# Attention and mixture-of-experts layer on one core: exponentials kept in SBUF, the maximum ahead of the preceding weighted sum, another order of the Q, K, V units, the norm in portions

## The chip, the cores and the metric

The kernel runs on one core of a Trainium2 chip. The metric is the device time of one execution in microseconds. Five engines work side by side, each through its own queue in order: TensorE (PE) multiplies, VectorE (DVE) and ScalarE (ACT) do element-wise work, GpSimd (POOL) does element-wise work in SBUF, and SyncE (SP) issues nearly all transfers. They wait for each other by semaphores. PSUM has eight banks of 128 x 512 words.

## The reference

Input x is (4, 1024, 512): four batches, 1024 tokens, width 512. One layer is computed: attention, norm, routed experts with a shared one, norm.

```
qkv = x @ w_qkv                       # 16 heads of width 128
scores = q @ k.T / sqrt(128)
probs = softmax(scores, axis=-1)
values = einsum('bhqk,bhkd->bhkd', probs, v)   # column sums of probs, times v
x = layernorm(x + values @ w_o)
x = layernorm(x + experts(x) + shared(x))      # 32 experts, 4 per token, capacity
```

Note `bhqk,bhkd->bhkd`: the query index is summed over probs alone. So attention needs for each head only the column sums of the softmax matrix (one number per key), which then multiply V.

## The kernel before, in words

All matrix work is done in three passes of split words: an operand is a rounded high part (HI) and the rest (LO = value - HI), and a product is HI.HI + HI.LO + LO.HI (`PASSES`). So every operand of PE has two makers: ACT rounds the high part, and POOL or DVE subtracts it to give the low part.

The attention goes through 64 heads (M = 64; 16 of each of 4 batches), in pairs of heads (`pair`, with `first_half` and `second_half`; in batch 0 `plain`, twice). A head has T = 8 score tiles of 128 queries x 1024 keys. Per tile t, PE makes the scores in two PSUM banks of four (`p_s`, alternating), `max_tile` on DVE takes the negated row maximum, ACT makes the exponential with its row sum, and `add_tile` on DVE takes the reciprocal and adds the row-weighted exponentials into a 128 x 1024 accumulator. What is left over partitions after eight tiles is folded: ACT copies the upper 64 partitions (`upper_cs`), POOL (DVE in batch 0) adds the lower 64 (`fold_cs`), ACT rounds (`hi_cs`), POOL subtracts (`lo_cs`), and PE sums over partitions and spreads the result with a matrix of ones (`spread`, at tile 3 of the next head). DVE multiplies with V (`times_v`), the pair's values are split, and PE multiplies with w_o (`out_tile`), which DVE adds to y (`add_y`).

In between, PE makes Q, K, V of the next heads. In batch 0 by plain products (`project`). Beside them POOL makes sums of weight blocks of later heads (`load_t` on SP, `sum_t` on POOL, `hi_t_sums` on ACT, `lo_t` on POOL, `store_t` on SP, through one buffer `t_own`), which go to DRAM (`w_jobs`); likewise sums of blocks of x (`load_x`, `sum_x`, `hi_x`, `lo_x`, `store_x_step`). In batches 1 to 3 these serve products with seven in place of eight block products (`unit`: P1 to P7 for Q and K of one head, and seven units for V of two heads, AT_V and AT_VE). A unit is 6 matmuls, accumulated in PSUM banks 4 to 7; between units of one bank ACT evacuates a partial result (`evac_u` to e_1, u_2, e_7 in rows_a; `evac_v`), and DVE or POOL adds the others (`add_block`, `add_v`).

The order of the work is written out by hand: each engine's function lists, for each tile t, what it does at that tile; nothing is planned at run time. Buffers in question:

- In batches 1 to 3 `exp_here` (L1406) writes the exponential back into the PSUM banks of the scores, and the weighted sums (L1902 the first of a head, L1905 the others) read them there. So the scores of tile t wait for the weighted sum of tile t - 2 (`dve_p`). In batch 0 `exp_tile` (L1398) writes to SBUF (`ex`, in rows_a), and the scores wait for the exponential alone (`act_e`).
- Two accumulators alternate there: one in `raws`, and `colsum`.
- The first norm of batch b - 1 (its `read_x`: mean and squares; `scale_x` on POOL; `write_x`: scaling; then `store_y`, `reload_y` on SP) is done in the second pair (k = 1) of batch b.

On DVE a tile is, in `first_half` before: add_tile of tile t - 1, then max_tile of tile t.

```
on_pe.wait_ge(dve_p if banked and not (...) else act_e, n * T + t - 1)   # before a tile's scores
```

## Time and profile before

| | us |
|---|---|
| median of 3 runs | 2806.37 (2805.11 to 2806.81) |
| the profiled execution | 2807.86 |
| its span | 2806.3 |
| PE busy | 2653.3 (95%) |
| DVE busy | 2080.3 (74%) |
| ACT busy | 1565.4 (56%) |
| POOL busy | 1300.6 (46%) |

The span runs from the first to the last instruction of the profiled execution. PE's busy time is modelled and overlapping matmuls count once, so 95% doesn't mean that PE issues at its full rate 95% of the time. Heads can be told apart in the trace by the score matmuls of line 2554: 48 to a head.

### The profile page before, as it was taken

How to read it: one execution, taken by the hardware profiler on the slowest of the kernel's cores; microseconds unless marked ns; L12 is line 12 of the kernel's file. 1: busy time of each engine (PE TensorE's matmuls, PEld its weight loads, DVE VectorE, ACT ScalarE, POOL GpSimd, SP SyncE). 2: the span in 40 equal slices, each digit the busy share in tenths (PEclk: the TensorE clock that was granted, in tenths of full speed). 3: DMA queues.
4: the chain of work that ended last, by engine and by line, in shares of the span. 5: the costliest groups of instructions: out<-in, count | busy, mean ns of one | idle time of the engine just before them, and what ended most of it. 6: DMA issues, size and time to landing. Idle time of an engine off the chain costs nothing.

```text
span 2806.3 us, 40617 instructions
## 1 busy us (share of the span) xinstructions
PE 2653.3 (95%) x12450; PEld 2159.3 (77%) x12450; DVE 2080.3 (74%) x3096; ACT 1565.4 (56%) x2627; POOL 1300.6 (46%) x1042
## 2 busy tenths in 40 slices
PE   9888888999899999999999999899999999999998
PEld 7777777877777777777777777677777788788887
DVE  6877777888788888877888888788888787533346
ACT  5555555656665566576565556756656442244434
POOL 3666666635455454544444444444444220266520
PEclk9999999999999999999999999999999999999999
DMA  5454455544534336445333463533334231288954
GB/s 176 136 171 143 142 169 155 169 170 129 166 112 117 113 103 215 115 120 162 110 103 103 117 205 105 173 98 103 106 101 156 82 128 55 68 253 253 249 162 150
DMA packets 351134, 397.51 MB, mean 142 GB/s; under 512 B 132780, under 2 KB 269996, under 8 KB 350496
## 3 DMA queue, kind: packets, MB, share of 16 engines
q1 hardware_dynamic: 340512, 383.92, 44.2%
q0 software_dynamic: 10496, 12.02, 2.3%
q8 instruction: 66, 1.08, 0.2%
q14 instruction: 60, 0.49, 0.1%
HBM read 299.58 MB, written 106.43 MB: 145 GB/s over the span
## 4 chain that ended last, share of the span: by engine, by line
PE 48%; issue 20%; DVE 19%; ACT 7%; POOL 4%; DMA 1%; ACTq 1%; DVEq 0%; SPq 0%; POOLq 0%
PE banks L2485 11%; PE banks L2554 9%; DVE neg_max L1885 8%; PE banks L2588 6%; PE banks L2394 5%; PE banks L2443 5%; PE banks L2472 4%; PE banks L2456 3%; ACT banks L1406 2%; PE banks L2403 2%; DVE raws L1905 2%; DVE inv L1892 1%; DVE colsum L1905 1%; DVE y_sb L1976 1%; POOL w_all L887 1%
## 5 line engine op out<-in xcount | busy, mean ns | idle before, releaser
L2485 PE MATMUL banks<-xt,w_all 128*128 128x512 f32 x3024 | 764.4, 396 | 77.3 <-ACT rows_a L1319 34.1
L2554 PE MATMUL banks<-qk 128*128 128x512 f32 x3072 | 781.6, 390 | 2.3 <-DVE colsum L1905 1.4
L2485 PEld LDWEIGHTS banks<-xt,w_all 128*128 128x128 f32 x3024 | 563.4, 189 | 234.5 <-ACT rows_c L1347 50.2
L1406 ACT ACTIVATE banks<-banks,neg_max 128x1024 f32<-128x1024 f32 x384 | 417.4, 1087 | 526.7 <-DVE neg_max L1885 523.9
L1885 DVE TENSOR_REDUCE neg_max<-banks 128x1 f32<-128x1024 f32 x512 | 623.5, 1218 | 82.3 <-PE banks L2554 80.4
L2554 PEld LDWEIGHTS banks<-qk 128*128 128x128 f32 x3072 | 574.7, 188 | 128.0 <-DVE colsum L1905 4.3
L2588 PE MATMUL banks<-wo_sb,val 128*128 128x512 f32 x1536 | 380.2, 392 | 8.7 <-DVE y_sb L1976 7.0
L2588 PEld LDWEIGHTS banks<-wo_sb,val 128*128 128x128 f32 x1536 | 289.5, 189 | 73.4 <-DVE y_sb L1976 7.9
L2472 PE MATMUL banks<-xt,w_all 128*128 128x512 f32 x1152 | 287.8, 401 | 6.5 <-DVE xt L2105 6.5
L1892 DVE RECIPROCAL inv<-rowsum 128x1 f32<-128x1 f32 x512 | 82.3, 161 | 278.1 <-ACT banks L1406 274.1
L952 POOL TENSOR_TENSOR qk<-rows_a,qk 128x512 fp32r<-128x512 f32 x144 | 186.5, 1295 | 199.9 <-ACT qk L1331 199.9
L2472 PEld LDWEIGHTS banks<-xt,w_all 128*128 128x128 f32 x1152 | 225.0, 195 | 55.4 <-POOL w_all L887 6.5
L899 POOL TENSOR_TENSOR cs<-folded,cs 64x1024 fp32r<-64x1024 f32 x63 | 150.5, 2389 | 221.1 <-ACT cs L1376 221.1
L1398 ACT ACTIVATE rows_a<-banks,neg_max 128x1024 f32<-128x1024 f32 x128 | 143.1, 1118 | 166.6 <-DVE neg_max L1885 166.1
L1905 DVE SCALAR_TENSOR_TENSOR colsum<-banks,inv,colsum 128x1024 f32<-128x1024 f32 x168 | 215.7, 1284 | 7.2
L1905 DVE SCALAR_TENSOR_TENSOR raws<-banks,inv,raws 128x1024 f32<-128x1024 f32 x168 | 215.7, 1284 | 6.4 <-DVE inv L1892 0.6
L939 POOL TENSOR_TENSOR folded<-folded,colsum 64x1024 f32<-64x1024 f32 x24 | 57.5, 2395 | 314.0 <-ACT folded L1368 314.0
L2394 PE MATMUL banks<-xt 128*128 128x512 f32 x768 | 181.8, 392 | 0.9 <-DVE raws L1848 0.5
L1976 DVE TENSOR_TENSOR y_sb<-y_sb,banks 128x512 f32<-128x512 f32 x256 | 168.2, 679 | 14.5 <-PE banks L2588 12.5
L2394 PEld LDWEIGHTS banks<-xt 128*128 128x128 f32 x768 | 142.5, 188 | 31.0 <-issue 1.7
L1905 DVE SCALAR_TENSOR_TENSOR colsum<-rows_a,inv,colsum 128x1024 f32<-128x1024 f32 x105 | 160.6, 1530 | 4.2
L1078 POOL DMA_INDIRECT acc_rows<-rows_b,who x64 | 93.3, 1458 | 92.0 <-DMA acc_rows<-rows_b,who 42.7
(238 smaller groups left out, 3540.2 us busy)
## 6 DMA issues: line engine op xcount, KB each, us to landing
w_all<-w_jobs SPq DMA_DIRECT2D x144, 512.0 KB, 3.7
w_all<-w_jobs SPq DMA_DIRECT2D x72, 768.0 KB, 4.4
w_jobs<-xt SPq DMA_DIRECT2D x96, 256.0 KB, 3.2
x_jobs<-xt SPq DMA_DIRECT2D x48, 448.0 KB, 5.6
xt<-x_jobs SPq DMA_DIRECT2D x21, 1024.0 KB, 6.7
w_jobs<-w_all SPq DMA_DIRECT2D x72, 256.0 KB, 3.5
...
```

The lines of the kernel that those rows point to most:

```text
L899: pool.tensor_tensor(cs[0:HP], folded[:], rounded(cs[0:HP]), ALU.subtract).then_inc(pool_cs, 1)
L952: pool.tensor_tensor(to[:, LO], f32, rounded(to[:, HI]), ALU.subtract).then_inc(pool_ql, 1)
L1398: act.activation(ex[:, t % 2], p_s[:, t % 2], ACT.Exp, bias=neg_max[:, t % 2], accum_out=rowsum[:, t % 2]).then_inc(act_e, 1)
L1406: act.activation(p_s[:, t % 2], p_s[:, t % 2], ACT.Exp, bias=neg_max[:, t % 2], accum_out=rowsum[:, t % 2]).then_inc(act_e, 1)
L1885: dve.tensor_reduce(neg_max[:, t % 2], p_s[:, t % 2], AX_X, ALU.max, negate=True)\
L1905: dve.scalar_tensor_tensor(out=dst, in0=of[:, t % 2], scalar=inv[:, t % 2], in1=dst, op0=ALU.mult, op1=ALU.add).then_inc(dve_p, 1)
L1976: dve.tensor_tensor(y_sb[:, j], y_sb[:, j], p_o[:, j % 2], ALU.add).then_inc(dve_y, 1)
L2394: ins = pe.matmul(p_f(f % 2, r), s_gu[:, a, k, at], parts[:, PARTS_OF[u], b, k], start=(k == 0 and (a, b) == PASSES[0]), stop=(k == KC - 1 ...
L2472: ins = pe.matmul(p_g[:, g % 2], w_sb[:, a, r, c], xt[:, PLAIN_AT[half][c // 2], b, c % 2], start=(c == 0 and (a, b) == PASSES[0]), stop=( ...
L2485: ins = pe.matmul(psum[:, bank], w_slot[pos % 7][:, a, c], x[:, half, c], start=(opens and c == 0 and (a, half) == PASSES[0]), stop=(c == ...
L2554: ins = pe.matmul(p_s[:, t % 2, keys], qk[:, par, Q, a, at], qk[:, par, K, b, keys], start=((a, b) == PASSES[0]), stop=((a, b) == PASSES[-1]))
L2588: ins = pe.matmul(p_o[:, j % 2], val2[:, r, a, at], wo_sb[:, r, b], start=(r == 0 and (a, b) == PASSES[0]), stop=(r == 1 and (a, b) == PAS ...
```

## The change

Nothing is computed otherwise. These things move:

1. Exponentials of batches 1 to 3 go to SBUF (`ex_late`, all of `raws`), `exp_here` is gone, all heads add into one accumulator `colsum`, and the scores wait for the exponential alone. The head's first weighted sum waits for POOL's fold of the head before.
2. On DVE max_tile of tile t comes ahead of add_tile of tile t - 1.
3. The units of Q and K are made in the order P1, P2, P7, P6, P4, P5, P3 instead of P1, P2, P6, P7, P5, P4, P3, with the evacuations and adds that belong to them; V's blocks are (1, 2, 4) early and (0, 3, 5, 6) in the main part instead of (1, 3, 5) and (0, 2, 4, 6). One of ACT's evacuations of V becomes a copy on DVE (`copy_v`).
4. Batch 0: on POOL `lo_t` of the head before and `lo_cs` come ahead of `sum_t`; on SP `store_w` and `load_w` come ahead of `store_t` and `load_t`; ACT rounds the sums at tiles 5 and 0 of the next head instead of 3 and 6.
5. The norm's reads and writes are spread over more tiles, and x's load in that pair comes after the reads, whose unused output now goes to x's buffer.
6. In the last head `spread` moves from tile 3 to tile 5 and `times_v` from 4 to 6.

The diff, cut to its core:

```diff
-    unused_row = raws[:, 2 * NB:3 * NB]
+    ex_late = raws[:].rearrange("p (a s) -> p a s", a=2)
-    colsums = (raws[:, 0:S], colsum[:])
-    QK_UNITS, V_EARLY, V_MAIN = 7, (1, 3, 5), (0, 2, 4, 6)
+    QK_UNITS, V_EARLY, V_MAIN = 7, (1, 2, 4), (0, 3, 5, 6)
-    P1, P2, P6, P7, P5, P4, P3 = range(7)
+    P1, P2, P7, P6, P4, P5, P3 = range(7)
...
         def plain(i, s):                                   # SP
             n = 2 * i + s
+            store_w(n + 1)
+            if n + 2 < H:
+                load_w(n + 2, n + 2)
             if 2 <= n - 1 <= H - 3:
                 store_t(n - 1, 1)
             if 2 <= n <= H - 3:
                 load_t(n, 0)
-            store_w(n + 1)
-            if n + 2 < H:
-                load_w(n + 2, n + 2)
...
         def second_half(b, k):                             # SP
-            if x_too:
+            if x_too and not k1:
                 load_x(b, k + 1, T * b + k + 1)
...
             if k1:
+                on_sp.wait_ge(act_q, 4 * TT * b)
+                load_x(b, k + 1, T * b + k + 1)
                 reload_y(b, 0)
...
         def plain(i, s):                                   # POOL
-            if sums:
-                sum_t(n, 0)
+            if late_sums:
+                lo_t(n - 1, 1)
             if not (is_first(i) and s == 0):
                 lo_cs(n - 1)
             if sums:
-                lo_t(n, 0)
+                sum_t(n, 0)
             if not end:
                 lo_w(n + 2, Q)
+            if x_step:
+                sum_x(0, i + s)
             if s == 0 and not is_first(i):
                 lo_wo(n - 1, 1)
             if sums:
-                sum_t(n, 1)
+                lo_t(n, 0)
             if not end:
                 lo_w(n + 2, K)
-            if x_step:
-                sum_x(0, i + s)
             if sums:
-                lo_t(n, 1)
+                sum_t(n, 1)
...
         def plain(i, s):                                   # ACT
-                if t in (3, 6) and sums:
-                    hi_t_sums(n, t // 6)
+                if t == 0 and (not isinstance(i, int) or 2 <= n - 1 <= H - 3):
+                    hi_t_sums(n - 1, 1)
+                if t == 5 and sums:
+                    hi_t_sums(n, 0)
...
         def first_half(b, k, i):                           # ACT
                 if t == 1:
                     evac_u(i, P1, m, 0)
+                    if k1:
+                        read_x(c, [0, 1])
...
                 if t == 4:
                     hi_val(n - 2, 0, i)
+                    if k1:
+                        read_x(c, [3])
+                        read_x(c + 1, [0])
                 if t == 5:
+                    evac_v(i, 3)
                     hi_block(i, 0, m, 1, 1)
-                    evac_v(i, 3)
...
-                exp_here(n, t)
-                if k1 and t < TT:
-                    read_x(c, [t])
+                exp_tile(n, t, ex_late)
...
         def second_half(b, k, i):                          # ACT
                 if t == 0:
-                    upper_cs(n - 1, colsums[0])
+                    upper_cs(n - 1)
+                    if k1:
+                        read_x(c + 1, [2])
+                        write_x(c, [0, 1])
                 if t == 1:
+                    evac_u(i, AT_S1 + P1, m, 0)
                     if not (b == 0):
-                        evac_v(i, 6)
-                    evac_u(i, AT_S1 + P1, m, 0)
+                        evac_v(i, 5)
+                    if k1:
+                        read_x(c + 1, [3])
+                        write_x(c, [2, 3])
...
-                if k1 and t == 1:
-                    write_x(c)
-                if k1 and t == 5:
-                    write_x(c + 1)
...
         def add_tile(n, t, of, by_pool=True):              # DVE
             if t == 0:
+                if by_pool:
+                    on_dve.wait_ge(pool_f, n - (H - 2))
+                else:
+                    on_dve.wait_ge(dve_cs, n)
+                dve.tensor_scalar(colsum[:], of[:, 0], inv[:, 0], None, ALU.mult).then_inc(dve_p, 1)
...
+        def copy_v(i):
+            on_dve.wait_ge(pe_u, units(i, AT_V + 2))
+            on_dve.wait_ge(dve_v, 2 * (2 * i))
+            dve.tensor_copy(v_sb[:, 1, NB:S], psum[:, 7]).then_inc(dve_ve, 1)
...
         def first_half(b, i):                              # DVE
-                if t == 0:
-                    add_tile(b, n - 1, T - 1, colsums[1], p_s)
-                else:
-                    add_tile(b, n, t - 1, colsums[0], p_s)
                 if t == 2:
                     add_block(i, 0, m, 0)
+                if t == 5:
+                    add_block(i, 0, m, 2)
+                if t == 7:
+                    copy_v(i)
                 max_tile(n, t)
...
                 if t == 6:
                     lo_block(m, 1)
+                if t > 0:
+                    add_tile(n, t - 1, ex_late)
...
         def second_half(b, i):                             # DVE
                 if t == 3:
-                    add_block(i, AT_S1, m, 1)
+                    add_block(i, AT_S1, m, 2)
...
                 max_tile(n, t)
                 if t == 1:
                     add_block(i, AT_S1, m, 0)
+                if t == 2:
+                    add_block(i, AT_S1, m, 1)
                 if t == 4:
                     lo_block(m, 0)
+                if t > 0:
+                    add_tile(n, t - 1, ex_late)
...
             elif j == P5:                                  # PE, qk_unit
-                on_pe.wait_ge(act_qe, 3 * q + 2)
+                on_pe.wait_ge(act_qe, 3 * q + 3)
             else:
-                on_pe.wait_ge(dve_qc, 3 * q + 2)
+                on_pe.wait_ge(dve_qc, 3 * q + 3)
...
         def v_unit(b, i, k):                               # PE
+            elif k < 3:
+                on_pe.wait_ge(act_ve, evacs(i, 3 + k))
             else:
-                on_pe.wait_ge(act_ve, evacs(i, 3 + k))
+                on_pe.wait_ge(dve_ve, i - (PB - 1))
...
         def scores(n, par, t, banked):                     # PE
-            on_pe.wait_ge(dve_p if banked and not (isinstance(n, int) and n == M - 1 and t >= 2) else act_e, n * T + t - 1)
+            on_pe.wait_ge(act_e, n * T + t - 1)
...
         def first_half(b, i):                              # PE
-                for j in {0: (P1,), 1: (P2,), 2: (P6, P7), 3: (P5,), 4: (P4,), 5: (P3,)}.get(t, ()):
+                if t == 5:
+                    v_unit(b, i, 1)
+                for j in {0: (P1,), 1: (P2,), 2: (P7, P6), 3: (P4,), 4: (P5,), 5: (P3,)}.get(t, ()):
                     qk_unit(b, i, 0, j)
-                if t >= 4:
+                if t in (4, 6, 7):
                     v_unit(b, i, t - 4)
```

## Rows read from the trace of the kernel before

**Rows 1.** The page, section 1: busy us, share of the span, instructions.
```profile
PE 2653.3 (95%) x12450; PEld 2159.3 (77%) x12450; DVE 2080.3 (74%) x3096; ACT 1565.4 (56%) x2627; POOL 1300.6 (46%) x1042
```

**Rows 2.** The chain of waits in time order, from 1250 us: start, us, what.
```profile
1260.99 1.37 PE banks L2554 x6
```

**Rows 3.** Windows at heads: length, busy PE, PEld, DVE, ACT, POOL, PEclk, DMA, GB/s.
```profile
80.00:122.50 42.50, 35.17 (x147) 28.37 (x147) 35.51 (x39) 25.08 (x39) 29.43 (x19) 0.92 0.51 149
200.20:233.30 33.10, 33.10 (x148) 27.41 (x147) 27.87 (x37) 20.53 (x31) 22.26 (x18) 1.00 0.46 140
233.30:277.80 44.50, 36.56 (x148) 29.30 (x147) 33.59 (x38) 22.35 (x34) 27.23 (x18) 0.88 0.56 164
464.60:507.80 43.20, 35.25 (x147) 28.44 (x146) 32.08 (x38) 22.28 (x34) 27.24 (x18) 0.92 0.57 169
606.00:639.00 33.00, 27.88 (x118) 21.43 (x118) 25.74 (x33) 21.34 (x34) 20.66 (x15) 1.00 0.32 96
1011.00:1076.80 65.80, 63.40 (x276) 50.98 (x275) 53.29 (x69) 39.52 (x64) 32.16 (x22) 1.00 0.39 110
1207.80:1243.40 35.60, 32.70 (x142) 26.08 (x142) 28.72 (x37) 29.67 (x58) 19.22 (x16) 1.00 0.40 108
1243.40:1284.20 40.80, 34.47 (x136) 27.25 (x135) 26.36 (x33) 26.66 (x47) 18.72 (x37) 0.92 0.56 188
```

**Rows 4.** PE's waits over the whole span: us in total, times, longest.
```profile
PE banks L2564 <- POOL cs L899: 40.8, 6, 7.6
PE banks L2485 <- ACT rows_a L1319: 34.1, 29, 1.8
PE banks L2485 <- ACT rows_c L1347: 30.3, 40, 3.9
```

**Rows 5.** Timeline of batch 0's even head from 233.3 us: start, us, engine, line.
```profile
242.51 1.05 ACT L1376 CAST cs<-folded 64x1024 fp32r<-64x1024 f32 x1 [1.14 <-DVE folded L1920]
...
248.14 0.72 POOL L906 TENSOR_TENSOR rows_c<-rows_c 128x256 f32<-128x256 f32 x1 [6.81 <-DMA rows_c<-in_w_qkv]
...
253.83 1.22 PE L2564 MATMUL banks<-cs,ones 128*128 128x512 f32 x2 [6.81 <-POOL cs L899]
...
254.85 3.62 PE L2472 MATMUL banks<-xt,w_all 128*128 128x512 f32 x8
```

**Rows 6.** Timeline of a second half with the norm.
```profile
737.50 2.92 ACT L1175 ACTIVATE y_sb<-y_sb,n_shift,n_scale 128x512 f32<-128x512 f32 x4
...
740.94 1.01 PE L2485 MATMUL banks<-xt,w_all 128*128 128x512 f32 x2 [3.31 <-ACT rows_c L1347]
```

**Rows 7.** Timeline of an ordinary first half, its last unit and its releaser.
```profile
976.06 0.58 ACT L1347 COPY v_sb<-banks 128x512 f32<-128x512 f32 x1
...
976.69 1.66 PE L2485 MATMUL banks<-xt,w_all 128*128 128x512 f32 x6 [0.39 <-ACT v_sb L1347]
```

**Rows 8.** Groups by line: busy us, mean ns of one, idle before.
```profile
L1905 DVE SCALAR_TENSOR_TENSOR colsum<-banks,inv,colsum 128x1024 f32<-128x1024 f32 x168 | 215.7, 1284 | 7.2
...
L1905 DVE SCALAR_TENSOR_TENSOR colsum<-rows_a,inv,colsum 128x1024 f32<-128x1024 f32 x105 | 160.6, 1530 | 4.2
...
L899 POOL TENSOR_TENSOR cs<-folded,cs 64x1024 fp32r<-64x1024 f32 x63 | 150.5, 2389 | 221.1 <-ACT cs L1376 221.1
```

**Rows 9.** DVE's instructions on rows_a: ns least/median/most, first and last start.
```profile
L1905 DVE SCALAR_TENSOR_TENSOR colsum<-rows_a,inv,colsum x105: 1283/1354/2926, 36.7 to 2214.9; 128x1024 f32<-128x1024 f32 x105
...
L1902 DVE TENSOR_SCALAR colsum<-rows_a,inv x15: 753/753/1600, 32.6 to 2189.0; 128x1024 f32<-128x1024 f32 x15
```

**Rows 10.** Timeline of DVE and POOL around one long weighted sum.
```profile
255.52 2.38 POOL L918 TENSOR_TENSOR xt<-rows_c,xt 128x1024 fp32r<-128x1024 f32 x1 [1.97 <-ACT xt L1294]
...
256.06 2.93 DVE L1905 SCALAR_TENSOR_TENSOR colsum<-rows_a,inv,colsum 128x1024 f32<-128x1024 f32 x1
```

**Rows 11.** Timeline of a tile where DVE waits for the scores.
```profile
245.50 1.52 PE L2554 MATMUL banks<-qk 128*128 128x512 f32 x6
...
247.06 1.23 DVE L1885 TENSOR_REDUCE neg_max<-banks 128x1 f32<-128x1024 f32 x1 [0.68 <-PE banks L2554]
248.20 0.68 DVE L1912 SCALAR_TENSOR_TENSOR qk<-banks,qk 128x512 fp32r<-128x512 f32 x1
```

224 lines of the change are left out of this document (108 added, 116 removed).

## The prediction

> **What bounds the kernel now.** I read the page first: TensorE (PE) is busy 95% of the span [rows 1], so the time can fall only by what PE waits, or by removing matmuls, and this change removes none. Busy time overstates PE, because matmuls overlap, so I priced one matmul from the chain of waits in order of time: six of them pass in 1.37 us [rows 2], 0.2265 us each by the length of undisturbed heads. With that price I cut the attention into heads at the first score matmul and laid windows over them [rows 3] (their matmul counts hold one or two of the neighbours at each edge; I use the program's counts). The reader is to see three kinds of excess there.
> - Batch 0, odd head: 146 matmuls cost 33.1 us and the window is 33.1 us long: no excess. The even head after it has as many and takes 44.5 us. The heads that begin at 80.0, 155.6, 233.3, 310.9, 387.4 and 464.6 us (heads 2 to 12, even) take 262.3 us together (six rows of that view, the first and the last of them shown), against 6 x 33.1 = 198.5: 63.8 us lost.
> - Batches 1 to 3, an ordinary pair of heads: 274 matmuls cost 62.1 us, the window is 65.8: 3.7 us lost, in nearly each of 24 pairs.
> - The pair in which the first norm of the preceding batch is done: 35.6 + 40.8 = 76.4 us, 10.6 more than an ordinary pair, three times (31.8 us). At the first head after batch 0, 116 matmuls cost 26.3 and take 33.0.
>
> From about 2213 us on (experts and last norm) the change touches nothing that PE waits for; I leave that part as it is.
>
> **Part A: order of POOL and SP in batch 0.** In the even heads PE's largest wait of the kernel stands: the spreading matmuls (L2564) wait for POOL's cs, 40.8 us in 6 waits [rows 4]. The stretch shows why [rows 5]: POOL idles 6.81 us until the weight blocks (rows_c) land, since the four subtractions of sum_t stand ahead of lo_cs in its queue; they were loaded late, because SP's load waits for lo_t of the head before, which stood last but one in POOL's queue. PE then idles 6.81 us, and the eight matmuls behind it take 3.62 us, 0.43 each, twice the usual time: the window's granted clock falls to 0.88, so part of them ran at 1.2 GHz, after PE had stood idle. Of such an 11 us, 7 are the wait, 2.8 the slow matmuls, and 1.4 a wait for DVE's y_sb later in the head, which is DVE's backlog from the stall.
> The change puts lo_t of the head before and lo_cs ahead of sum_t. What lo_cs waits for is then ACT's high half of cs, at 9.2 us of the head (242.51 in rows 5), and POOL's work before it: lo_wo until about 7.7, lo_t 2.4 us to 10.1, lo_cs 2.4 us [rows 8] to 12.5. PE wants it after three tiles of 18 matmuls and a score, 66 - 6 = 60 matmuls or 13.6 us. Cover: 1.1 us; it is gone if lo_t comes later. lo_t waits for ACT's rounding, moved to tile 0, that for the second sum_t, that for the load which SP issues only after lo_t of the first block. I step through it: first lo_t ends near 26 us, loads issued to 28, landed near 30.4 (about 4.3 us after the first issue), sum_t 3.2 us and its queue to 34, which is 1 us into the next head, ACT idle then until its exponential at 2.8. So it fits, with little to spare. SP's stores and weight loads, now ahead of the store and load of blocks, take some 5 us of issue at the head's start, when the block store cannot go anyway. POOL is busy 22.3 and 27.2 of 33 and 44 us in such heads [rows 3], 75% when the pair shrinks. I take 0.6 us of new wait per head: 63.8 - 3.8 = **-60 us** (bounds: -64 with none, -35 if half of each wait comes back).
>
> **Part B: norm in portions.** In the pair with the norm ACT is busy 29.7 + 26.7 = 56.4 us against 39.5 [rows 3], so 16.9 us for 16 reading and 8 writing instructions. It isn't the sum that hurts (ACT has 9 us left) but the lumps: four writes in a row, 2.92 us, ahead of one evacuation, after which PE had idled 3.31 us [rows 6]; the granted clock is 0.92 in that head [rows 3]. The change writes two at a time and spreads the reads. The rests that I find, by laying the new order out tile by tile: two reads at tile 4 of the first half put the evacuation that V's second unit needs some 2 us late; two writes and a read at tiles 0 and 1 of the second half cost another 2 to 3; about 1 later. That is 5.5 of 10.6, and no wait long enough to bring the slow matmuls: 3 x 5.1 = **-15 us** (bounds -26 and 0). The load of x now waits for the reads (its buffer takes their unused output); SP holds back only itself, and the transfer has three tiles until hi_x, moved to tile 7.
>
> **Part C: exponentials in SBUF, maximum first, units in another order.** Today's 3.7 us per pair are four waits of PE's unit matmuls for ACT's evacuations (rows_a and rows_c in rows 4), the last of the first half in rows 7. ACT is not full; it holds an exponential ahead of each evacuation, the exponential waits for the maximum, and the maximum stands behind reciprocal and weighted sum of the tile before, which wait for *its* exponential. Max first takes 1.4 us (0.2 + 1.2 of spacing) out of that loop, and two evacuations move ahead in ACT's order. All four waits (0.5 to 1.5 us) go. What is late next? I lay out the new order with: maximum starts 1.56 us after the scores' first matmul (245.50 to 247.06), holds DVE 1.14 (to 248.20) [rows 11]; reciprocal plus sum 1.4; a 512-wide add or copy 0.6 to the next, 0.68 to its end [rows 11].
> - *V's fourth unit* in the first half now waits for copy_v, which DVE does after max 6, lo_block and sum 5: 1.56 + 1.14 + 0.6 + 1.4 + 0.68 + 0.1 = 5.5 us after scores 6 begin. PE is there after scores 6, V's third unit, scores 7: 18 matmuls, 4.1 us. It waits 1.4, and 0.1 to restart. Today's wait at this place is 0.39 [rows 7].
> - *P3 in the second half* waits for the add of P5, now behind max 2, the add of P4 and sum 1: 5.8 us after scores 2 begin, where PE comes at 5.4: 0.4 + 0.1.
> - *DVE's price.* A sum costs 1284 ns from PSUM; from SBUF a head's first one costs 753 [rows 9], but the others take 1530 on average [rows 8], between 1283 and 2926 [rows 9]. The long ones overlap POOL: the one of 2.93 us starts at 256.06 while POOL works until 257.90, and ends 1.09 us after that [rows 10]. So each sum begun under a POOL instruction waits for its end. I take +0.25 us (1530 - 1284) for 14 sums of a pair, -1.06 for the two first ones, +0.68 for copy_v: 53.3 + 3.1 = 56.4 us of DVE in a pair of 65: DVE does not bound. ACT has 26 us a pair free [rows 3] and gives up one copy: nothing there.
> - *Where such a wait meets PE.* lo_cs (2.4 us) runs in the second half about when sum 1 is due; up to 1.2 us on the P3 wait, I take 0.6. In the first half POOL's 1.3 us pieces touch sum 5: 0.2, and P6 behind P1's evacuation 0.2.
> - *Added wait.* One colsum for all heads: the first sum of a head waits for POOL's fold, and max, adds and all of DVE behind it. Last sum, ACT's copy 1.05, fold 2.4: 3.6 us; DVE has max 0, adds and max 1 between, over 3.6 us in both halves. Nothing, or 0.5 if POOL is held.
>
> Sum per pair: 1.5 + 0.5 + 0.6 + 0.2 + 0.2 = 3.0 after, 3.7 to 3.8 before: -0.8, times 24 = **-19 us**. Bounds: all four waits go and nothing comes, -3.3 x 24 = -79; every sum waits like the longest of 2926, the fourth rival's +13 each. I stand nearer the small gain since both new waits follow from the order of DVE alone.
>
> The Trainium skill, page "SBUF — State Buffer", section "Who interferes with whom", has a rule that speaks against this part: a DVE instruction with two SBUF inputs contends with a GpSimd instruction that reads SBUF, with one PSUM operand it doesn't, and the first to start holds the port to its end. The trace agrees on both sides (1284 on average from PSUM, up to 2926 from SBUF). By the row's mean the pair loses 3.5 us of DVE slack, by the rule's worst case that of the fourth rival.
>
> **Part D: edges.** In the first head after batch 0 the scores no longer wait for the weighted sums: of its 6.7 us I take 2.5 back; the last head's spread moves where it waits for nobody: 0.5. **-3 us** (0 to -6).
>
> Sum: -60 - 15 - 19 - 3 = -97. The profiled execution took 2807.86 us (span 2806.3 and 1.56 around it), so 2710.9; the median is 1.5 less: **2709 us**.
>
> **Rivals.**
> 1. *PE's floor in the pairs.* The new waits are hidden after all and pairs take 62.5: 2806.4 - 60 - 15 - 79 - 3 = 2649. For it: max first removes the longest loop. Against: the two sums above. Chance 0.22.
> 2. *The pairs give nothing or lose.* Contention moves the waits for copy_v and P3 over 2 us, where today the slow matmuls appear (3.31 us of idling in rows 6); pairs take 65.8 to 67.8: 2728 to 2776, say 2745. Chance 0.22.
> 3. *Batch 0 keeps half its stall*, as lo_t comes late behind the chain of load, sum and rounding, with 1.1 us of cover: 35 instead of 60, 2734. Chance 0.08.
> 4. *DVE becomes the bound by POOL's port, slower than before.* Place: the 16 sums of a pair. Each waits 1.64 us more (2926 - 1284) at worst, 26 us a pair; 53.3 - 0.4 + 26 = 79 us, +13 x 24 = +317: 3045. It decides from a pair of 69.1 on, where 3.3 x 24 eats A, B and D; that is 16 us of waiting in a pair, 1 us per sum, four times the measured mean; POOL is busier in batch 0, where that mean is from, than in the later pairs (32.2 of 65.8). Chance 0.05.
> 5. *The change doesn't do what it says*: ACT's order holds the exponentials back, and A is hidden by another wait: within 0.2%. Chance 0.02.
>
> The forecast has the remaining 0.41. The range goes from rival 1 to the middle of rival 2: 2645 to 2765; the forecast's own is 2690 to 2725. A difference under 0.2% (5.6 us) can't be told from none here; faster by more: 0.41 + 0.22 + 0.22 + 0.08 = 0.93; same 0.02; slower 0.05.
>
> **What would show it.** A: waits of L2564 for POOL gone from PE's list, even heads at 33 to 34 us, clock 1.00. B: second half of the norm pairs under 38 us. C: PE's units waiting for DVE's v_sb copy about 1.4 us once a pair, and for rows_a's add in the second half; sums from SBUF near 1.5 us mean; exponentials right after maxima; a pair near 65. I am wrong if a pair takes 62.5 (new waits hidden) or over 67 (port), or if even heads of batch 0 stay over 36.

## The result, and the profile after

| | before | after |
|---|---|---|
| median, us | 2805.82 (4 runs) | 2781.43 (4 runs, 2772.5 to 2785.49) |
| the profiled execution | 2807.86 | 2785.49 |
| after / before | | 0.9909 [0.9882, 0.9935] |

The change makes the kernel 24 us faster, a quarter of the 97 us forecast; 2709 was forecast and 2781 lies above the range. The page's section 1 of after, against [rows 1]: DVE gained 80 us of work and POOL 107. PE waits less in sum, but in the profiled executions it has 94 us at half clock (1.2 GHz) against 70 before. After's four runs, 2785.49, 2784.64, 2772.5 and 2778.22 us, were granted 0.984, 0.984, 0.989 and 0.988 of the full clock over their spans; 0.005 of the span is 14 us, so by this estimate most of their scatter of 13 us is the clock, and the profiled run is the slowest of the four.

```profile
PE 2655.4 (95%) x12450; PEld 2179.1 (78%) x12450; DVE 2160.8 (78%) x3120; ACT 1556.8 (56%) x2603; POOL 1407.8 (51%) x1042
```

PE's waits of after over the whole span (us in total, times, longest), against [rows 4]: L2578 is the spreading matmul, L2602 `out_tile`, L2497 a unit, L2568 the scores.

```profile
PE banks L2497 <- DVE v_sb L2017: 49.6, 24, 2.9
PE banks L2578 <- POOL cs L904: 12.8, 5, 2.7
PE banks L2497 <- DVE rows_a L1940: 12.5, 24, 1.2
PE banks L2568 <- POOL qk L957: 11.4, 3, 4.0
PE banks L2602 <- POOL wo_sb L898: 7.6, 4, 3.0
```

The two old waits for ACT's evacuations (34.1 and 30.3 us) are gone, as forecast, the third (11.2 us, for v_sb) as well. The one for POOL's cs has shrunk from 40.8 to 12.8 us and is not gone, and four others have come. Windows of after at heads (columns as in [rows 3]): an odd and two even heads of batch 0, the first head after it, an ordinary pair, the two halves of a norm pair.

```profile
116.70:149.80 33.10, 33.10 (x148) 27.41 (x147) 28.80 (x37) 20.44 (x31) 24.32 (x19) 1.00 0.58 177
149.80:191.70 41.90, 36.45 (x147) 29.33 (x146) 34.12 (x38) 22.21 (x34) 30.98 (x19) 0.92 0.53 157
443.00:485.30 42.30, 36.69 (x148) 29.48 (x147) 34.40 (x39) 22.20 (x34) 31.00 (x19) 0.92 0.51 154
586.70:619.40 32.70, 28.41 (x117) 22.46 (x116) 30.50 (x36) 22.06 (x35) 24.48 (x16) 0.96 0.42 125
988.20:1053.50 65.30, 62.70 (x275) 51.28 (x274) 55.33 (x71) 39.12 (x63) 35.74 (x22) 1.00 0.38 110
1186.50:1225.00 38.50, 32.58 (x142) 25.96 (x140) 32.59 (x41) 29.77 (x58) 22.03 (x25) 0.99 0.40 120
1225.00:1259.10 34.10, 33.46 (x134) 27.14 (x135) 24.84 (x30) 26.25 (x45) 22.51 (x28) 0.91 0.61 201
```

Cutting both traces at the first score matmul of each head puts the 22.8 us by which the spans differ where they belong:

| | before | after | difference | forecast |
|---|---|---|---|---|
| even heads 2 to 12 | 262.3 | 238.9 | -23.4 | -60 |
| rest of batch 0 | 318.6 | 322.0 | +3.4 | 0 |
| three norm pairs | 228.3 | 218.1 | -10.2 | -17 |
| 19 other pairs | 1248.0 | 1255.0 | +7.0 | -15 |
| first pair after batch 0 | 65.7 | 64.1 | -1.6 | -3 |
| start, last heads, the rest | | | +2.0 | -1 |

### The profile page after: what moved, and what is told of

It reads as the page before. It is cut to its first block, busy times and chain, and to the rows that moved or that the text cites. A ratio compares the mean times of both kernels' runs of the same rounds, so it can differ in the third digit from the quotient of the medians.

```text
span 2783.5 us, 40658 instructions
## 1 busy us (share of the span) xinstructions
PE 2655.4 (95%) x12450; PEld 2179.1 (78%) x12450; DVE 2160.8 (78%) x3120; ACT 1556.8 (56%) x2603; POOL 1407.8 (51%) x1042
## 3 DMA queue, kind: packets, MB, share of 16 engines
q8 instruction: 66, 1.08, 0.2%
## 4 chain that ended last, share of the span: by engine, by line
PE 66%; issue 5%; DVE 3%; POOL 1%; ACT 1%; DVEq 0%; ACTq 0%; POOLq 0%
PE banks L2497 21%; PE banks L2568 15%; PE banks L2602 9%; PE banks L2406 6%; PE banks L2455 5%; PE banks L2468 3%; PE banks L2415 3%; PE banks L2330 1%; PE banks L2578 1%; PE banks L2442 1%; DVE rows_a L1940 1%; DVE qk L1949 1%; DVE v_sb L2017 1%; PE banks L2354 0%; DVE colsum L1910 0%
## 5 line engine op out<-in xcount | busy, mean ns | idle before, releaser
L2497 PE MATMUL banks<-xt,w_all 128*128 128x512 f32 x3024 | 760.8, 395 | 66.5 <-DVE v_sb L2017 49.6
L2568 PE MATMUL banks<-qk 128*128 128x512 f32 x3072 | 792.3, 394 | 11.7 <-POOL qk L957 11.4
L2497 PEld LDWEIGHTS banks<-xt,w_all 128*128 128x128 f32 x3024 | 570.6, 190 | 207.0 <-DVE v_sb L2017 59.8
L1407 ACT ACTIVATE raws<-banks,neg_max 128x1024 f32<-128x1024 f32 x392 | 438.5, 1119 | 508.2 <-DVE neg_max L1893 504.9
L2568 PEld LDWEIGHTS banks<-qk 128*128 128x128 f32 x3072 | 584.3, 190 | 136.8 <-POOL qk L957 12.7
L1910 DVE SCALAR_TENSOR_TENSOR colsum<-raws,inv,colsum 128x1024 f32<-128x1024 f32 x343 | 525.3, 1531 | 13.5
L2602 PE MATMUL banks<-wo_sb,val 128*128 128x512 f32 x1536 | 381.0, 392 | 13.9 <-POOL wo_sb L898 7.6
L2602 PEld LDWEIGHTS banks<-wo_sb,val 128*128 128x128 f32 x1536 | 289.4, 189 | 79.1 <-issue 10.7
L944 POOL TENSOR_TENSOR folded<-folded,colsum 64x1024 f32<-64x1024 f32 x49 | 117.3, 2394 | 376.7 <-ACT folded L1378 376.7
L957 POOL TENSOR_TENSOR qk<-rows_a,qk 128x512 fp32r<-128x512 f32 x144 | 204.6, 1428 | 133.1 <-ACT qk L1341 133.1
L1407 ACT ACTIVATE rows_a<-banks,neg_max 128x1024 f32<-128x1024 f32 x120 | 134.1, 1117 | 131.0 <-DVE neg_max L1893 130.1
L1910 DVE SCALAR_TENSOR_TENSOR colsum<-rows_a,inv,colsum 128x1024 f32<-128x1024 f32 x105 | 174.6, 1663 | 4.2
L948 POOL TENSOR_TENSOR val<-rows_b,val 128x1024 fp32r<-128x1024 f32 x48 | 140.7, 2932 | 22.7 <-ACT val L1399 22.7
L1378 ACT COPY folded<-colsum 64x1024 f32<-64x1024 f32 x63 | 66.1, 1049 | 122.3 <-DVE colsum L1910 121.9
## 6 DMA issues: line engine op xcount, KB each, us to landing
xt<-x_jobs SPq DMA_DIRECT2D x21, 1024.0 KB, 10.8
```

The costliest lines, as they stand in the source:

```text
L948: pool.tensor_tensor(val2[:, r, LO], val[:, r], rounded(val2[:, r, HI]), ALU.subtract)\
L957: pool.tensor_tensor(to[:, LO], f32, rounded(to[:, HI]), ALU.subtract).then_inc(pool_ql, 1)
L1407: act.activation(to[:, t % 2], p_s[:, t % 2], ACT.Exp, bias=neg_max[:, t % 2], accum_out=rowsum[:, t % 2]).then_inc(act_e, 1)
L1910: dve.scalar_tensor_tensor(out=colsum[:], in0=of[:, t % 2], scalar=inv[:, t % 2], in1=colsum[:], op0=ALU.mult, op1=ALU.add).then_inc(dve_p, 1)
L2497: ins = pe.matmul(psum[:, bank], w_slot[pos % 7][:, a, c], x[:, half, c], start=(opens and c == 0 and (a, half) == PASSES[0]), stop=(c == ...
L2568: ins = pe.matmul(p_s[:, t % 2, keys], qk[:, par, Q, a, at], qk[:, par, K, b, keys], start=((a, b) == PASSES[0]), stop=((a, b) == PASSES[-1]))
```

## Experiments

All are edits of the kernel after, except `e7_max_first_psum`, an edit of the kernel before. Times are medians, ratios to the kernel before with their interval; "heads" and "pairs" are cut as above.

### 1. The copy of V earlier: `e1_copy_early`

DVE's copy moves from behind the sum of tile 5 to ahead of it.

```diff
@@ DVE, first half
-                if t == 7:
-                    copy_v(i)
                 max_tile(n, t)
...
                 if t == 6:
                     lo_block(m, 1)
+                    copy_v(i)
                 if t > 0:
                     add_tile(n, t - 1, ex_late)
```

> The changed kernel with copy_v done at tile 6, behind lo_block and ahead of the weighted sum of tile 5, instead of at tile 7 behind that sum. Theory (PE waits once a pair for DVE's order max 6, lo_block, sum 5, copy_v): the wait of the unit matmuls for v_sb, 2.1 to 2.3 us once a pair, goes, first halves fall from 34.1 us to about 32, a pair from 65.3 to 63.1; 24 pairs give 50 to 60 us, about 2725. Rival (DVE is the bound through the sums from SBUF, and the wait only moves): the pair stays over 64.5 and the gain is under 20 us, 2762 or more.

Measured: 2753.3 us, 0.9815 [0.9798, 0.9831], 28 us under after. PE's waits:

```profile
PE banks L2567 <- POOL qk L957: 20.7, 6, 5.1
PE banks L2496 <- ACT rows_a L1329: 18.7, 18, 1.1
PE banks L2496 <- DVE rows_a L1940: 14.3, 24, 1.2
```

The wait of 49.6 us is gone and the first halves fall from 34.15 to 31.8 us. But the second halves rise from 31.15 to 32.6: the next unit's evacuation by ACT, which the longer first half had covered, is now late 18 times. So the wait is real, but of the 2.35 us that the first half gains the second gives 1.45 back: a typical pair takes 64.4 us, between the 63.1 expected and the rival's 64.5, and the 28 us lie between the two as well. The pairs that took 66.9 us in after gain most: of the six ordinary ones five now take 64.3 or 64.4. In the norm pairs hardly anything is gained: there the wait for POOL's qk grows from 3.7 to 5.1 us.

### 2. Batch 0's order undone: `e2_batch0_back`

SP, POOL and ACT in batch 0 as in the kernel before, the rest as after.

```diff
@@ POOL, plain
-            if late_sums:
-                lo_t(n - 1, 1)
+            if sums:
+                sum_t(n, 0)
             if not (is_first(i) and s == 0):
                 lo_cs(n - 1)
...
@@ SP, plain
-            store_w(n + 1)
-            if n + 2 < H:
-                load_w(n + 2, n + 2)
             ...                      # store_t, load_t
+            store_w(n + 1)
+            if n + 2 < H:
+                load_w(n + 2, n + 2)
```

> The changed kernel with the order of batch 0 (SP, POOL, ACT) as before. Theory (batch 0 brings 20 us of the whole gain): even heads 2 to 12 take 262 us again instead of 239, the first sixteen heads 581 instead of 561, the whole about 2801. Rival (the order of batch 0 is worth the 60 us that I forecast and something else of the change takes 40 away in batch 0): over 2820.

Measured: 2799.7 us, 0.9978 [0.9968, 0.9988]. The even heads take 262.3 us again and POOL's cs is waited for 40.4 us in 6 waits. Part A is worth 18 us by the medians and 19 by the sixteen heads of batch 0, not 60; the rest of the change is worth the remaining 6.

### 3. The norm in lumps: `e3_norm_back`

```diff
@@ ACT, first half
+                if k1 and t < TT:
+                    read_x(c, [t])
+                if k1 and t in (5, 6):
+                    read_x(c + 1, [t - 5])
@@ ACT, second half
+                if k1 and t < 2:
+                    read_x(c + 1, [2 + t])
+                if k1 and t == 1:
+                    write_x(c)
+                if k1 and t == 5:
+                    write_x(c + 1)
-                ...                  # the same calls one or two at a time
```

> The changed kernel with ACT's reading and writing of the norm at the places of before (one read behind the exponential of each tile, four writes in a row at tiles 1 and 5 of the second half). Theory (portions bring 3.4 us a norm pair): the three norm pairs take about 228 us instead of 218, the whole about 2791. Rival (with maxima ahead ACT has room for the lumps): the three pairs within 3 us of 218, no difference that can be measured.

Measured: 2790.1 us, 0.9949. The three norm pairs take 233.8 us against 218.1: the portions are worth 15.7 us in the new order, where about 10 were expected (8.7 by the medians; batch 0 of this run took 5 us less than after's, with the same code). All of it lies in the second halves, 39.5 us against 34.2; the first ones take 38.4 either way.

### 4. Sum ahead of the maximum, in SBUF and in PSUM: `e4_sum_first`, `e7_max_first_psum`

The first undoes the order of DVE's two instructions in after; the second makes the order of after in the kernel before, whose exponentials are in PSUM. With the two kernels they fill a table of two by two. Within a row only that order differs. The rows differ in more than the place of the exponentials: in after the units come in another order, V's copy is DVE's and there is one accumulator.

```diff
@@ e4_sum_first, both halves
+                if t > 0:
+                    add_tile(n, t - 1, ex_late)
                 max_tile(...)
-                if t > 0:
-                    add_tile(n, t - 1, ex_late)
@@ e7_max_first_psum, both halves
-                    add_tile(b, n, t - 1, colsums[0], p_s)
                 max_tile(...)
+                if t > 0:
+                    add_tile(b, n, t - 1, colsums[0], p_s)
```

> The changed kernel with the weighted sum of tile t - 1 ahead of the maximum of tile t again in batches 1 to 3; exponentials stay in SBUF, the scores wait for the exponential alone, copy_v stands ahead of sum 6 at tile 7, so no longer behind sum 5 and max 7 but behind max 6 and lo_block. Theory (max first shortens the loop that ACT's evacuations hang on, 1.4 us): the waits of unit matmuls for ACT come back, 3 to 4 us a pair, the wait for copy_v goes (-2.3), pairs at 65 to 67, the whole 2775 to 2820. Rival (the loop never mattered, only the order of units and evacuations did): pairs at 63, about 2725.

> The kernel before with one thing of the change: in batches 1 to 3 the maximum of tile t ahead of the weighted sum of tile t - 1, exponentials still in PSUM. Theory (the two parts need each other: with exponentials in PSUM the scores of tile t + 1 wait for the sum of t - 1, now behind max t, 1.56 + 1.14 + 1.4 us after scores t begin, 4.1 and more where an add stands between): pairs at 68 to 76 us instead of 65.8, the whole 2860 to 3050. Rival (max first helps by itself, as ACT's evacuations come earlier): pairs under 65.

Measured: 2871.7 us, 1.0241 [1.0224, 1.0259], and 3044.3 us, 1.0845. An ordinary pair, us:

| | sum first | maximum first |
|---|---|---|
| exponentials in PSUM | 65.8 (before) | 76.6 |
| exponentials in SBUF | 69.9 | 65.3 (after) |

The first was expected at 2775 to 2820 us, with the copy's wait gone, and missed: that wait stayed. The second came in the range expected, its pair just above it. So the maximum first costs 10.8 us a pair in PSUM and gains 4.6 in SBUF. The 4.1 us by which the sum first in SBUF is over the kernel before are not the price of SBUF alone: 2.1 us of each pair are the wait for the copy, which the kernel before leaves to ACT. PE's waits with the sum first in SBUF, then with the maximum first in PSUM:

```profile
PE banks L2497 <- ACT rows_a L1329: 46.6, 32, 2.3
PE banks L2497 <- DVE v_sb L2017: 44.7, 23, 2.1
PE banks L2497 <- ACT rows_a L1357: 13.4, 23, 2.0
```

```profile
PE banks L2554 <- DVE raws L1905: 139.3, 111, 2.1
PE banks L2554 <- DVE colsum L1905: 68.4, 72, 1.4
```

In PSUM the scores of tile t need the bank that the sum of tile t - 2 reads, and with the maximum ahead that sum is late at half of the tiles (201 waits in 384 tiles). In SBUF that tie is gone; but with the sum first a sum that is longer than in PSUM (1475 ns on average) stands ahead of the maximum, the exponential behind it, and ACT's evacuation behind that, and the waits for ACT are back.

### 5. Which queue holds batch 0: `a1_wo_after_cs`, `a2_sp_back`, `a3_wo_before_sum`, `a4_wo_all`

```diff
@@ a1_wo_after_cs: POOL, plain, even head
-            if s == 0 and not is_first(i):
-                lo_wo(n - 2, 0)
             ...                      # lo_t(n - 1, 1); lo_cs(n - 1)
+            if s == 0 and not is_first(i):
+                lo_wo(n - 2, 0)
@@ a2_sp_back: SP, plain
-            store_w(n + 1)
-            if n + 2 < H:
-                load_w(n + 2, n + 2)
             ...                      # store_t, load_t
+            store_w(n + 1)
+            if n + 2 < H:
+                load_w(n + 2, n + 2)
@@ a3_wo_before_sum: POOL, plain; sum_t(n, 0) behind the second lo_wo in even heads
-            if sums:
+            if s == 1 and sums:
                 sum_t(n, 0)
             ...                      # lo_w(n + 2, Q); lo_wo(n - 1, 1)
+            if s == 0 and sums:
+                sum_t(n, 0)
@@ a4_wo_all: a1 and a3, and on SP the second load_wo of an even head ahead of store_t and load_t
```

> The changed kernel; on POOL in batch 0 the first lo_wo (of head n - 2) of an even head moves from ahead of lo_t and lo_cs to behind lo_cs. Theory (the spreading matmuls wait 2.3 to 2.9 us in seven even heads because lo_wo, 2.3 us, lo_t, 2.9, and lo_cs, 3.3, stand in a row from 7.7 us of the head on, each lengthened by the port it shares with DVE): the wait of L2577 or so for POOL's cs goes from 12.8 to under 3 us, 10 to 17 us in batch 0, unless the later wait for lo_wo of head n - 1 grows by the same. Rival (ACT's rounding of cs or of the block sums is what comes late, not lo_wo): the wait stays within 1 us per head.

> The changed kernel with SP's order of batch 0 as before (store_t and load_t ahead of store_w and load_w), POOL and ACT as changed. Theory (the second wait of an even head, out_tile for lo_wo of head n - 1, comes from load_t issued at 18.8 us of the head, behind 9 us of issues of store_w and load_w): load_t is issued near 14 us, POOL's wait for the blocks falls from 8 to 3 us, the out_tile wait goes, 9 to 15 us less in batch 0. Rival (load_w is then late, ACT waits for it as before the change and holds the exponentials): batch 0 no shorter or up to 10 us longer.

> The changed kernel; on POOL in even heads of batch 0 lo_w of Q and lo_wo of head n - 1 stand ahead of the first sum_t, which waits for the transfer. Theory (lo_wo only suffers from its place behind sum_t): the waits of the output matmuls for POOL's wo_sb, 7.6 us in 4, and DVE's y_sb backlog go, 8 to 15 us less in batch 0. Rival (w_o itself is loaded behind load_t by SP, at 21.9 us of the head, so lo_wo cannot be earlier and now holds sum_t and ACT's rounding up): batch 0 the same or longer.

> The changed kernel, batch 0 alone: first lo_wo of an even head behind lo_cs (as a1), lo_w of Q and the second lo_wo ahead of the first sum_t (as a3), and SP loads w_o ahead of store_t and load_t in even heads. Theory (what a3 lacked was the load of w_o, 21.7 us of ACT's waits): PE waits neither for cs nor for wo_sb in batch 0, 10 to 16 us less than a1's 2768.6. Rival (the chain load, sum, rounding, subtraction through the one block buffer is the bound, and the wait moves to ACT's rounding of sums and to the exponentials behind it): within 5 us of a1.

Measured: 2768.6 (0.9861 [0.9843, 0.9878]), 2791.1 (0.9944), 2779.4 (0.990) and 2768.4 us (0.9864). Even heads 2 to 12: 230.5, 249.3, 240.0 and 226.4 us against 238.9. PE's waits in batch 0 with the first edit:

```profile
PE banks L2602 <- POOL wo_sb L898: 16.4, 6, 2.8
PE banks L2578 <- POOL cs L904: 3.1, 5, 1.1
```

The wait for cs falls from 12.8 to 3.1 us, that for wo_sb grows from 7.6 to 16.4, and still 13 us are gained. One part of it is the clock: a window over the even head that begins at 368.5 us has it at 1.00, as three of the six even heads here and two of them in after; no window of the six is under 0.95, where after has two of 0.92.

```profile
368.50:407.10 38.60, 34.27 (x148) 27.11 (x147) 34.04 (x38) 22.01 (x35) 26.09 (x17) 1.00 0.51 149
```

SP's order of before loses 10 us where 9 to 15 were expected to be gained: the weights then come late, and ACT waits 70.6 us for them in batch 0 instead of 10.1. Moving the second lo_wo ahead of sum_t moves the wait to ACT, which waits 61.9 us for POOL's sums instead of 24.1, and nothing is gained. All together, a4 was expected 10 to 16 us under a1 and is level with it: PE waits for wo_sb no more, but ACT waits 64.2 us for POOL's sums.

### 6. The second half: `e5_copy_p3`, `e6_max0_first`

```diff
@@ e5_copy_p3: e1, and in the second half, t == 2
                 ...                  # add of P4
+                    add_block(i, AT_S1, m, 2)      # of P5, from behind sum 1
                 add_tile(n, t - 1, ex_late)
@@ e6_max0_first: e5, and in both halves, t == 0
                 max_tile(...)
+                    add_tile(n - 1, T - 1, ex_late)
-                ...                  # that call ahead of the maximum
@@ and on ACT, both halves: upper_cs(n - 1) at t == 1, behind exponential 0, instead of at t == 0
```

> The changed kernel with copy_v ahead of sum 5 (as e1_copy_early) and, in the second half, the add of P5 at tile 2 behind the add of P4, ahead of sum 1, instead of at tile 3 behind it. e1 left two waits in second halves, 1.25 us before P6 (for ACT's evacuation of P1, behind exponential 0) and 0.7 us before P3 (for DVE's add of P5). Theory (they are separate): the wait for rows_a of DVE, 14 us in 24, goes, 12 to 16 us less than e1, about 2739. Rival (the time is caught by the next wait, as with e1, where 2.3 us taken away gave 0.9): under 5 us less.

> e5 and in addition the maximum of a head's tile 0 ahead of the last weighted sum of the head before, and on ACT the copy of colsum's upper half behind exponential 0 instead of ahead of it. Theory (P6's 1.25 us hang on exponential 0, that on the copy and on max 0, both on sum 7): the evacuation of P1 comes 2 us earlier, the wait goes, second halves fall from 32.6 to about 30.5, pairs to 62.5, the whole 2700 to 2720. Rival (the fold of colsum, now 1.5 us later, holds the first sum of the head and all of DVE behind it): pairs stay at 64 and PE waits for DVE.

Measured: 2755.0 us (0.9811) and 2762.4 us (0.9834), no better than the copy alone, where 2739 and 2700 to 2720 were expected. In e5 the wait for P5's add (14.3 us in experiment 1) is gone and another stands at the product with w_o, in e6 a larger one (first e5, then e6):

```profile
PE banks L2600 <- DVE rows_b L1969: 19.6, 21, 1.0
```

```profile
PE banks L2600 <- DVE rows_b L1968: 25.5, 21, 1.4
```

Both are waits for `times_v`, which DVE does later for what was put ahead of it. The window of e6 over one second half shows that DVE has 3 us left there, so it is late by its order and not for want of time:

```profile
951.80:985.10 33.30, 31.08 (x136) 25.04 (x136) 30.18 (x36) 19.04 (x31) 18.35 (x13) 1.00 0.33 91
```

### 7. POOL's work taken away: `f1_narrow_late`, `f2_narrow_b0`

Both leave out part of the low parts that POOL subtracts; waits and transfers stay.

```diff
@@ f1_narrow_late: lo_val and lo_block on POOL, batches 1 to 3
-   val2[:, r, LO], val[:, r], ...
+   val2[:, r, LO, 0:8], val[:, r, 0:8], ...
-   to[:, LO], f32, ...
+   to[:, LO, 0:8], f32[:, 0:8], ...
@@ f2_narrow_b0: in batch 0's loop lo_w makes one of C = 4 blocks, lo_t 128 of 1024 columns
```

> The changed kernel, leaving work out: in batches 1 to 3 POOL makes only 8 of 512 (of 1024) columns of the low parts of Q, K and of the values; all waits stay. That takes 10.9 us of POOL's reading in SBUF out of a pair and touches no other engine. Theory (of the 2.1 us that V's fourth unit waits for copy_v, 1.3 are DVE's own order and 0.8 the port, by which sum 5 takes 2.2 us instead of 1.3 under POOL's low part of K): sum 5 takes 1.28, the wait falls to 1.2 or 1.4, sums from raws from 1531 to under 1400 ns, a pair from 65.3 to 64.0 to 64.5, the whole 2755 to 2768. Rival (DVE's order alone sets it): wait and pair within 0.3 us of the changed kernel's.

> The changed kernel, leaving work out: in the loop of batch 0 (heads 4 to 13) POOL makes only a quarter of the weights' low parts and an eighth of those of the block sums; all waits and transfers stay. That takes about 6 us of POOL's work out of a head. Theory (the first wait of an even head is POOL's queue from 7.7 us on, the second hangs on SP's issue of load_t at 18.8 us): PE's wait for cs in four or five even heads goes, 12 to 3 us; the one for wo_sb stays within 2 us per head; the even heads come down by 2 to 4 us each, the whole 2765 to 2775. Rival (POOL's work, not SP and the transfer, is the bound of batch 0): both waits go, even heads at 33 to 34, the whole under 2755.

Measured: 2744.3 us (0.9775 [0.9760, 0.9790]), lower than the 2755 to 2768 expected, and 2752.8 us (0.9809 [0.9794, 0.9824]), where the rival had said under 2755. f1 first: DVE's sums from 620 to 2100 us in after, then in f1 (busy us, mean ns, idle before):

```profile
L1910 DVE SCALAR_TENSOR_TENSOR colsum<-raws,inv,colsum 128x1024 f32<-128x1024 f32 x309 | 473.4, 1532 | 12.3
```

```profile
L1911 DVE SCALAR_TENSOR_TENSOR colsum<-raws,inv,colsum 128x1024 f32<-128x1024 f32 x316 | 429.8, 1360 | 12.5
```

DVE's instruction is the same; only what POOL does beside it became shorter, and it takes 172 ns less. PE's waits in f1:

```profile
PE banks L2498 <- DVE v_sb L2018: 32.7, 24, 1.5
...
PE banks L2498 <- DVE rows_a L1941: 10.6, 22, 1.2
```

In an ordinary pair the sum ahead of the copy takes 1.50 us against 2.21 and the copy is waited for 1.40 us against 2.11; the wait of the scores for POOL's qk is gone. The ordinary second halves, in after 31.15 us and 32.5 to 32.8 in six of seventeen, are 31.1 us without exception: behind the copy's waits, 1.5 us at most here, PE is never slow. Pairs take 64.6 us. Not all is gain: the norm's second halves rise from 34.2 to 36.5. f2: the spreading matmuls no longer wait for cs and the even heads take 213.4 us, 25.5 less than in after. PE's waits from 25 to 560 us:

```profile
PE banks L2604 <- POOL wo_sb L899: 4.5, 3, 1.7
PE banks L2570 <- ACT rows_a L1409: 1.8, 1, 1.8
```

So what holds back batch 0 is more POOL's amount of work in an even head than one place in its order: the best order tried (a4) takes 12.5 us off the even heads, less work in the order of after 25.5, to within 15 us of the 198.5 in which PE waits for nothing. Whether it is POOL's time alone or also the contention that it brings to DVE, this run doesn't separate.

### 8. The two that paid, together: `c3_copy_wo`

The edits of `e1_copy_early` and `a1_wo_after_cs`.

> The changed kernel with copy_v ahead of sum 5 (e1) and in batch 0 the first lo_wo behind lo_cs (a1): the two edits with a gain of their own, in different batches. Theory (they add up): 28 and 13 us less than 2781, 2738 to 2743, the fastest of all. Rival (a1's gain was the scatter of batch 0 from run to run): as e1, 2750 to 2755.

Measured: 2740.75 us (2738.31 to 2744.41), 0.9769 [0.9756, 0.9783], as expected. It gains 41 us on after, where the two alone gained 28 and 13, and it beats both kernels. Its longest waits:

```profile
PE banks L2567 <- POOL qk L957: 20.7, 6, 5.2
PE banks L2496 <- ACT rows_a L1329: 18.9, 19, 1.1
PE banks L2601 <- POOL wo_sb L898: 17.2, 7, 3.3
```

## Why the prediction was wrong

**Part A is the step that failed: "I take 0.6 us of new wait per head".** The six even heads lie 40.3 us over 198.5, where 3.8 were forecast: PE idles 26.7 us in them and has 20.4 us at half clock. The forecast's -60 came to -20 over batch 0; 40 of the 74 us between forecast and the profiled execution lie here, and the bound of -35 was too narrow. What the even head that begins at 149.8 us shows (the timeline of after; SPq is SP issuing DMAs):

```profile
157.47 2.28 POOL L898 TENSOR_TENSOR wo_sb<-wo_raw,wo_sb 128x512 fp32r<-128x512 f32 x1 [0.21 <-ACT wo_sb L1299]
...
159.72 2.85 POOL L923 TENSOR_TENSOR xt<-rows_c,xt 128x1024 fp32r<-128x1024 f32 x1
...
162.53 3.32 POOL L904 TENSOR_TENSOR cs<-folded,cs 64x1024 fp32r<-64x1024 f32 x1
163.61 2.20 SPq L537 DMA_DIRECT2D raws<-in_w_qkv  x3
165.86 2.67 SPq L577 DMA_DIRECT2D w_jobs<-xt  x4
...
166.10 1.22 PE L2578 MATMUL banks<-cs,ones 128*128 128x512 f32 x2 [2.58 <-POOL cs L904]
...
168.57 3.00 SPq L567 DMA_DIRECT2D rows_c<-in_w_qkv  x4
...
173.99 0.74 POOL L911 TENSOR_TENSOR rows_c<-rows_c 128x256 f32<-128x256 f32 x1 [8.14 <-DMA rows_c<-in_w_qkv]
...
181.09 2.24 POOL L898 TENSOR_TENSOR wo_sb<-wo_raw,wo_sb 128x512 fp32r<-128x512 f32 x1
...
183.47 4.35 PE L2602 MATMUL banks<-wo_sb,val 128*128 128x512 f32 x12 [2.87 <-POOL wo_sb L898]
```

1. *POOL's three instructions end 16 us into the head, not at 12.5.* The list was right: lo_wo, lo_t, lo_cs. But I had lo_wo done at 7.7 us, as in the kernel before, and it begins there, behind sum_t, lo_w and lo_x of the head before; and lo_t and lo_cs take 2.85 and 3.32 us instead of 2.4 each. DVE's sums are in SBUF in batch 0 before as after; with the new order POOL's instructions fall beside other DVE work in SBUF (from 25 to 580 us lo_wo went from 1430 to 2206 ns on average, lo_cs from 2371 to 2798). The cover of 1.1 us becomes a wait of 2.58.
2. *A wait that I did not look for.* The load of the blocks is issued at 168.57, 18.8 us into the head, since SP has 7 us of weight transfers (3.35, 1.55 and 2.20) and 2.67 of stores ahead of it, and begins on them only 7.5 us into the head, when POOL's lo_x of the head before is done and its block can be stored (1.24 us). POOL idles 8.14 us with sum_t, and what stands behind sum_t in its queue is the second lo_wo, which PE needs at 180.6: 2.87 us more. I counted what sum_t no longer stands ahead of (lo_cs), and not what it still stands ahead of.
3. *The slow clock stayed.* The window's granted clock is 0.92, as it was before the change in such heads [rows 3]; one long wait became two, and the slow matmuls came with each. So it is in this head and in the one at 443.0 us. In the heads at 224.8 and 298.7 PE waits for cs (2.61 and 2.71 us, slow matmuls behind both) and later for DVE's val and y_sb (2.6 and 2.3); in the one at 372.5 the clock stays at 1.00 behind 2.36 us, and the one at 80.9 has no wait for cs.

Experiment 5 separates the two waits and experiment 7 names what both rest on. That lo_t would fit behind load, sum and rounding (rival 3) was a doubt about the right chain, at a chance of 0.08 and with 35 us kept; 20 were.

**Part B: right.** 15 us were forecast for the portions, and undoing them costs 15.7 (experiment 3). The second halves fell from 40.8 to 34.2 us, under the 38 named as the sign. That the norm pairs gained 10.2 only is part C's doing: their first halves rose from 35.6 to 38.5, with the norm in lumps too (38.4). The timeline of after at the end of such a half shows POOL's last subtraction for K late, behind lo_val in its queue, and the next head's scores behind it:

```profile
1220.36 2.36 POOL L948 TENSOR_TENSOR val<-rows_b,val 128x1024 fp32r<-128x1024 f32 x1
1222.68 2.24 POOL L957 TENSOR_TENSOR qk<-rows_a,qk 128x512 fp32r<-128x512 f32 x1
...
1224.97 2.93 PE L2568 MATMUL banks<-qk 128*128 128x512 f32 x6 [3.71 <-POOL qk L957]
```

With POOL's low parts narrowed (experiment 7) these first halves take 34.5 us. I had looked in them for ACT alone.

**Part C: each wait where it was put, and the port's price put on the wrong one.** Forecast: four waits go, the copy costs 1.5 us and 0.2 of the port, P3 0.5 and up to 0.6 of the port. The four went. P3 waits 12.5 us in 24 waits, 0.52 each: its 0.5, without the 0.6. The copy waits 2.07 on average, in this pair 2.13 (timeline of after):

```profile
1016.05 1.23 DVE L1893 TENSOR_REDUCE neg_max<-banks 128x1 f32<-128x1024 f32 x1 [0.45 <-PE banks L2568]
...
1017.19 0.68 DVE L1949 TENSOR_TENSOR qk<-banks,qk 128x512 fp32r<-128x512 f32 x1
...
1017.83 1.29 POOL L957 TENSOR_TENSOR qk<-rows_a,qk 128x512 fp32r<-128x512 f32 x1
1017.98 2.23 DVE L1910 SCALAR_TENSOR_TENSOR colsum<-raws,inv,colsum 128x1024 f32<-128x1024 f32 x1
1019.07 2.26 POOL L966 TENSOR_TENSOR v_sb<-v_sb,rows_c 128x512 f32<-128x512 f32 x1
...
1020.13 0.68 DVE L2017 COPY v_sb<-banks 128x512 f32<-128x512 f32 x1
...
1020.86 1.65 PE L2497 MATMUL banks<-xt,w_all 128*128 128x512 f32 x6 [2.13 <-DVE v_sb L2017]
```

The order is the one laid out: maximum, lo_block, sum, copy. The sum begins 0.15 us behind a POOL instruction and takes 2.23 us, 0.95 more than the 1.28 of an undisturbed one, where 0.2 was allowed for the port. In a norm pair, at the same place, POOL has small instructions there:

```profile
1217.66 1.29 DVE L1910 SCALAR_TENSOR_TENSOR colsum<-raws,inv,colsum 128x1024 f32<-128x1024 f32 x1
...
1219.61 1.66 PE L2497 MATMUL banks<-xt,w_all 128*128 128x512 f32 x6 [1.19 <-DVE v_sb L2017]
```

The wait follows this one sum: where it takes 1.28 to 1.31 us (three pairs), 2.2 (nineteen) and 3.03 or 3.04 (two), the copy is waited for 1.2, 2.1 and 2.9. So the term that was mis-sized is the port's 0.2 on this sum; with an undisturbed sum the wait is 1.2, under the 1.5 forecast. The mean of the sums was forecast to 2 ns (1530; measured 1531 over 343), but a mean says nothing of one sum: this one meets POOL in each ordinary pair. The Trainium skill, "SBUF — State Buffer", section "Who interferes with whom", says that a DVE instruction with two SBUF inputs contends with a GpSimd one that reads SBUF; by that rule sum 5 had to be placed against POOL's timeline, and the rows of the ordinary pair agree, as do the 172 ns of experiment 7. That the first to start holds the port to its end, which the prediction also took from there, the section says of DVE's 2-port modes; the last part below has what the trace shows of it for these sums.

An undisturbed pair takes 65.3 us, half a microsecond less than before, where 65.0 was forecast. That this became +7 over all is nearly all the slow clock, which eight of the nineteen pairs have: a window over the unit matmuls behind a wait of 2.11 us, and one behind a wait of 2.13 (columns as in [rows 3]; PEclk follows POOL's count):

```profile
1292.06:1294.79 2.73, 2.73 (x7) 2.14 (x8) 2.69 (x4) 1.21 (x2) 1.71 (x2) 0.55 0.08 17
1020.86:1022.50 1.64, 1.64 (x7) 1.38 (x8) 1.60 (x3) 0.53 (x1) 1.64 (x2) 1.00 0.11 23
```

The pairs with the first kind take 66.9 to 67.2 us (mostly 34.3 + 32.6). Rival 2 named this, from waits over 2 us on; I had costed this one at 1.5. Its price for the pairs (65.8 to 67.8) holds the mean of the nineteen, 66.05. Its 2745 for the whole still had A at 60. (The range of 2645 to 2765 was said to end in the middle of this rival; the middle of 2728 and 2776 is 2752.)

**Part D.** The first head after batch 0 kept 32.7 us of its 33.0 in place of 30.5, as the copy's wait of 2.9 us fell into it, and slow matmuls behind it; in experiment 1 it takes 30.5, the forecast. The tail is as before.

DVE is not the bound (55.3 us of a pair forecast at 56.4), so rival 4 fell; rival 1 fell with the waits for copy and P3. Where the 74 us are: A 40, part C in the 19 pairs 22 and in the norm pairs 8, the edges 5, and B 1 the other way. Of the forecast's terms A is off most, and the port on the copy's sum, with the slow clock that its wait brings, is second.

What stays open: with the same code in batch 0 its 16 heads took 555.7 to 560.9 us in seven kernels' profiles (after, e1, e3, e4, e5, e6, f1). PE idles 25.1 to 29.6 us in them and has 17.1 to 23.9 us at half clock; without the idle time and half of the slow time all seven lie between 519.5 and 521.2. So the scatter is in waits and clock, as that of after's runs is in the clock; why these fall differently with the same code wasn't isolated. Nor were POOL's sums moved to another engine, which experiment 7 suggests for batch 0.
